# Windowed attention on one core: exponentials by block with row sums, halves of a strip on separate partitions, the normalising product on POOL

## The chip, the cores and the metric

The kernel runs on one NeuronCore of a Trainium2 chip. Its five engines are PE (matrix products), DVE (vector), ACT (activations), POOL (general purpose) and SP (here only a DMA queue). The metric is the device time of one execution in microseconds (us), lower is better.

## The reference, cut to what matters

Input is a batch of 8 images of 56 x 56 tokens with 64 channels. A convolution block, an attention layer, a graph and mixture-of-experts layer follow each other. The change lies in the attention layer alone:

```python
qkv = (x @ W_qkv.T).reshape(Bb, Nn, 3, 8, 8)           # 8 heads of 8 channels
attn = einsum('bhqd,bhkd->bhqk', q, k) * (scale * temperature[0])
mask = local_mask(Nn)                                  # rows and columns at most 3 apart
attn = softmax(where(mask, attn, -inf), axis=-1)
out = einsum('bhqk,bhkd->bhqd', attn, v)
return out @ W_proj.T + b_proj                         # added to the tokens
```

## The kernel before, in words

The program is a row of phases with a barrier between them: `conv_phase`, `attention_phase`, `index_phase`, `table_phase`, `edge_phase`, `join_phase`, `output_phase`. Only `attention_phase` (L787 to L1075) and a mask table are touched.

The phase works through 112 strips (8 images of 14 strips; a strip is 4 rows of 56 tokens). A strip is 14 blocks of 4 x 4 tokens. A block's queries, spread over 8 heads, make 128 rows, and its keys are a window of 10 x 10 = 100 tokens. For each strip:

- SP (`loads`, L869) brings keys, mask features, queries and, in ten transfers, the values.
- POOL (`spread_q`, L898) multiplies the queries by the head mask into `q_exp` (64 x 1792), so that one product gives the scores of all heads of a block. The mask features add -2^100 for keys outside of the window.
- PE (`scores`, L933) writes the scores of 14 blocks to three PSUM banks `psS` (5, 5 and 4 blocks).
- DVE (`subtract_max`, L1025) takes each row's maximum and subtracts it, from PSUM to `prob`, bank by bank. ACT (`exponentials`, L991) takes the exponential of a bank in place.
- PE (`turn_probs`, L947) transposes `prob` block by block to `psP`; ACT (`copy_probs`, L998) copies that to `prob_t`.
- PE (`weigh_values`, L957) multiplies by `val` (100 x 128 for a block: 64 value channels and 64 ones, which give the row sums) to `psO`, in four groups of 4, 4, 4 and 2 blocks. The result holds all heads' products; `own_head` (L1036) on DVE multiplies by the head mask, adds over heads, takes the reciprocal of the sums (L1049) and multiplies (L1052) into `o_ch`.
- PE (`project`, L968) applies the output weights; DVE (`residual`, L1056) adds the tokens; POOL (`add_bias`, L907) adds the bias and stores.

Each engine runs its own program in order, and semaphores join them. What sets the order is each engine's `step`, with i the strip:

```python
pe:   turn_probs(i); scores(i+1); project(i-1); weigh_values(i)
act:  load_t1(i); copy_probs(i); exponentials(i+1)
dve:  subtract_max(i+1); residual(i-1); own_head(i)
pool: spread_q(i+2); add_bias(i-1)
```

`own_head(i)` waits for `weigh_values(i)` group by group. `scores(j)` waits for `spread_q(j)`. `spread_q(j)` waits for `scores(j-2)` and for its queries. fp32 products are issued by the compiler as two instructions on PE each, transposes as one: 28 for the scores, 28 for the values, 14 transposes and 4 for the projection in a strip.

Of the kernel before, what the change touches and what calls it, by code (L numbers as in the profile page):

```python
# [72 lines left out]
def mask_features():  # L73
# [15 lines left out]
    for j in range(QROWS):  # L89
        queries[j, :, :, j, :] = 1  # L90
    for x in range(W):
        queries[QROWS + x % 16, x // QCOLS, :, :, x % QCOLS] = 1
# [694 lines left out]
def attention_phase(nc, io, t1_dram, q_dram, kpad_dram, vpad_dram, t2_dram):  # L787

    with ExitStack() as ctx:
# [8 lines left out]

        ident = sb("a_ident", [128, 128])
        headmask = sb("a_headmask", [2 * C, HEADS])  # L800
        wproj = sb("a_wproj", [C, C])
        bproj = sb("a_bproj", [TOK, C])
# [5 lines left out]
        val = sb2("val", [KEYS, BLOCKS, 2 * C])  # L808
        t1 = sb2("t1", [TOK, 2, C])
        prob = sb2("prob", [128, BLOCKS * KEYS])  # L810
        mx = sb2("mx", [128, BLOCKS])
        prob_t = sb("prob_t", [KEYS, BLOCKS, 128])
        own = sb2("own", [2 * C, 4, HEADS, QB])
        sums = sb("sums", [2 * C, BLOCKS, QB])
        inv = sb("inv", [C, BLOCKS, QB])
        o_ch = sb2("o_ch", [C, SPIX])
        t2a = sb2("t2a", [TOK, 2, C])
        t2 = sb2("t2", [TOK, 2, C])
# [6 lines left out]
        GROUPS = [(0, 4), (4, 8), (8, 12), (12, 14)]  # L825

        const_in = sem("const_in")
        ones_set = sem("ones_set")
# [4 lines left out]
        exp_q = sem("exp_q"); s_ready = sem("s_ready"); mx_done = sem("mx_done"); sub_done = sem("sub_done")  # L833
        exp_done = sem("exp_done"); pt_ready = sem("pt_ready"); pt_done = sem("pt_done")
        pv_ready = sem("pv_ready"); own_done = sem("own_done"); summed = sem("summed"); inv_done = sem("inv_done")
        o_done = sem("o_done"); pr_ready = sem("pr_ready")
        t2a_done = sem("t2a_done"); t2_done = sem("t2_done")

        t1_view = t1_dram.rearrange("(i r p) c -> i p r c", r=2, p=TOK)
        t2_view = t2_dram.rearrange("(i r p) c -> i p r c", r=2, p=TOK)  # L840
        consts = [(ident[:], "ident"), (headmask[0:C], "headmask"), (headmask[C:2 * C], "headmask"), (wproj[:], "wproj")]
# [8 lines left out]
        def every_strip(eng, step):  # L850

            step(Strip(0, 0), True, False)
            step(Strip(0, 1), False, False)
            with eng.Fori(1, PAIRS - 1) as turn:
                step(Strip(turn, 0), False, False)
                step(Strip(turn, 1), False, False)
            step(Strip(PAIRS - 1, 0), False, False)
            step(Strip(PAIRS - 1, 1), False, True)

        with nc.Block() as block:  # L860
            @block.sync
            def _(sp):
                for dst, name in consts:
                    sp.dma_start(dst, io[name]).then_inc(const_in, 16)
                sp.dma_start(bproj[:], io["bproj"].rearrange("(a b) -> a b", a=1).to_broadcast([TOK, C])).then_inc(const_in, 16)
# [3 lines left out]
                def loads(n, s, par, i):  # L869

                    wait(sp, s_ready, 3 * i - 3)
                    sp.dma_start(keys[par][0:C, :],
                                 kpad_dram[:, n, bass.ds(s * QROWS, WIN), :].rearrange("c y x -> c (y x)")).then_inc(kq_loaded[par], 16)
                    sp.dma_start(keys[par][C:KROWS, :], io["kfeat"][bass.ds(s, 1)].rearrange("o f x -> (o f) x")).then_inc(kq_loaded[par], 16)
                    wait(sp, exp_q, i - 1)
                    sp.dma_start(q[par][:], q_dram[:, n, bass.ds(s * SPIX, SPIX)]).then_inc(kq_loaded[par], 16)
                    wait(sp, pv_ready, 4 * i - 4)
                    for ky in range(WIN):
                        sp.dma_start(val[par][ky * WIN:(ky + 1) * WIN, :, 0:C], windows(n, s * QROWS + ky)).then_inc(v_loaded[par], 16)

                sp.wait_ge(ones_set, 2)
                for par in range(2):
                    loads(0, par, par, par)
                with sp.Fori(1, STRIPS // 2) as pair:
                    for par in range(2):
                        loads(0, pair * 2 + par, par, pair * 2 + par)
                with sp.Fori(1, N) as n:
                    with sp.Fori(0, STRIPS // 2) as pair:
                        for par in range(2):
                            loads(n, pair * 2 + par, par, n * STRIPS + pair * 2 + par)  # L890

            @block.gpsimd
            def _(pool):
                for par in range(2):
                    pool.memset(val[par][:], 1.0).then_inc(ones_set, 1)  # L895
                pool.wait_ge(const_in, 16 * N_CONST)

                def spread_q(st):  # L898
# [5 lines left out]
                                       headmask[0:C].unsqueeze(1).unsqueeze(3).to_broadcast([C, BLOCKS, HEADS, QB]),  # L904
                                       ALU.mult).then_inc(exp_q, 1)

                def add_bias(st):  # L907
                    i, par = st.i, st.par
                    pool.wait_ge(t2a_done, i + 1)
                    wait(pool, t2_stored[par], 16 * (st.turn))  # L910
                    pool.tensor_tensor(t2[par][:], t2a[par][:], bproj[:].unsqueeze(1).to_broadcast([TOK, 2, C]), ALU.add)\
                        .then_inc(t2_done, 1)
                    pool.wait_ge(t2_done, i + 1)
                    pool.dma_start(t2_view[i], t2[par][:]).then_inc(t2_stored[par], 16)
# [9 lines left out]
                every_strip(pool, step)  # L924
                add_bias(Strip(PAIRS - 1, 1))
                for par in range(2):
                    pool.wait_ge(t2_stored[par], 16 * PAIRS)

            @block.tensor
            def _(pe):  # L930
                pe.wait_ge(const_in, 16 * N_CONST)

                def scores(st):  # L933
# [3 lines left out]
                    for bank, (a, b) in enumerate(BANKS):  # L937
                        wait(pe, sub_done, 3 * i - 3 + bank + 1)
# [18 lines left out]
                def weigh_values(st):  # L957
                    i, par = st.i, st.par
                    pe.wait_ge(v_loaded[par], 16 * WIN * (st.turn + 1))
                    for k, (a, b) in enumerate(GROUPS):  # L960
                        pe.wait_ge(pt_done, 4 * i + k + 1)
                        wait(pe, own_done, 4 * i + k - 1)
                        for blk in range(a, b):
                            m = pe.matmul(psO[k % 2][:, (blk - a) * 128:(blk - a + 1) * 128], val[par][:, blk, :],  # L964
                                          prob_t[:, blk, :], start=True, stop=True)
                        m.then_inc(pv_ready, 1)

                def project(st):  # L968
# [3 lines left out]
                    for r in range(2):  # L972
                        m = pe.matmul(psM[0:TOK, SPIX + r * C:SPIX + (r + 1) * C], o_ch[par][:, r * TOK:(r + 1) * TOK], wproj[:],
                                      start=True, stop=True)
                    m.then_inc(pr_ready, 1)

                def step(st, first, last):
                    turn_probs(st)
                    if not last:
                        scores(st.step(1))  # L980
# [3 lines left out]

                scores(Strip(0, 0))
                every_strip(pe, step)
# [3 lines left out]
            def _(act):  # L990
                def exponentials(st):  # L991
                    i, par = st.i, st.par
                    for bank, (a, b) in enumerate(BANKS):
                        act.wait_ge(sub_done, 3 * i + bank + 1)
                        p = prob[par][:, a * KEYS:b * KEYS]
                        act.activation(p, p, ACT.Exp).then_inc(exp_done, 1)

                def copy_probs(st):  # L998
                    i, par = st.i, st.par
                    for k, (a, b) in enumerate(GROUPS):  # L1000
                        act.wait_ge(pt_ready, 4 * i + k + 1)
                        if k == 0:
                            wait(act, pv_ready, 4 * i)
# [3 lines left out]
                def load_t1(st):  # L1007
                    i, par = st.i, st.par
                    wait(act, t2a_done, i - 1)
                    act.dma_start(t1[par][:], t1_view[i]).then_inc(t1_loaded[par], 16)  # L1010

                def step(st, first, last):
                    load_t1(st)
                    copy_probs(st)
                    if not last:
                        exponentials(st.step(1))

                exponentials(Strip(0, 0))
                every_strip(act, step)

            @block.vector
            def _(dve):
                dve.wait_ge(const_in, 16 * N_CONST)

                def subtract_max(st):  # L1025
                    i, par = st.i, st.par
                    for bank, (a, b) in enumerate(BANKS):
                        dve.wait_ge(s_ready, 3 * i + bank + 1)
                        s = psS[bank][:, 0:(b - a) * KEYS].rearrange("p (b k) -> p b k", k=KEYS)
                        dve.tensor_reduce(mx[par][:, a:b], s, AX.X, ALU.max).then_inc(mx_done, 1)  # L1030
                        dve.wait_ge(mx_done, 3 * i + bank + 1)
                        dve.tensor_tensor(prob[par][:, a * KEYS:b * KEYS].rearrange("p (b k) -> p b k", k=KEYS), s,
                                          mx[par][:, a:b].unsqueeze(2).to_broadcast([128, b - a, KEYS]), ALU.subtract)\
                           .then_inc(sub_done, 1)

                def own_head(st):  # L1036

                    i, par = st.i, st.par
                    for k, (a, b) in enumerate(GROUPS):
                        n = b - a  # L1040
                        dve.wait_ge(pv_ready, 4 * i + k + 1)
# [929 lines left out]
```

## Time and profile before

| what | value |
|---|---|
| median of 3 runs | 6784.15 us (6781.37 to 6784.29) |
| the profiled execution | 6765.31 us |
| its span in the profile | 6763.6 us |
| PE, DVE, ACT, POOL busy, share of the span | 50%, 55%, 14%, 46% |
| mean granted clock of PE | 0.648 of full speed |
| attention, first `q_exp` to last `t2a` | 1541.9 to 2920.5 us |

The profile gives, for each engine, what it did and what ended each idle time. Its clock column is PE's granted clock as a share of 2.4 GHz: 1.00 is 2.4 GHz and 0.50 is 1.2 GHz. A line number names the line of the kernel that issued an instruction.

### The profile page before, as it was taken

The numbers are of one execution on the slowest core, as the hardware profiler recorded it, in microseconds if no ns is written. First come the engines' busy times: TensorE is split into PE (matmuls) and PEld (weight loads), VectorE is DVE, ScalarE is ACT, GpSimd is POOL, SyncE is SP. The second block draws the span as 40 slices with busy tenths as digits, with TensorE's granted clock in tenths as the row PEclk, the third lists the DMA queues.
The fourth block names the chain that finished last, engine by engine and source line by source line (L and its number), as shares of the span: only waits on it lengthen the run. The fifth ranks groups of instructions, "written<-read, shape, count | busy, mean of one in ns | idle before, by whom it ended". The sixth has DMA issues, their size and how long they took to land. (4 is left out here: it accounts for less than half of the span.)

```text
span 6763.6 us, 59936 instructions
## 1 busy us (share of the span) xinstructions
PE 3366.5 (50%) x16368; PEld 2375.4 (35%) x16368; DVE 3733.1 (55%) x5332; ACT 962.3 (14%) x1813; POOL 3137.9 (46%) x2752
## 2 busy tenths in 40 slices
PE   2788878767888888845444400572222222222000
PEld 0344434336777777734333300341111111111000
DVE  4988888857999999942999400321111111111129
ACT  0112222212333333312000000110000000000000
POOL 0000000003333333312888777677777777777545
PEclk9878787768988989855555555555555555555555
DMA  6455555542222222233100100121111111111125
GB/s 136 81 85 86 85 85 85 84 71 65 63 60 61 60 60 61 60 84 76 31 8 8 20 8 4 56 79 32 32 32 32 32 32 32 30 30 28 25 71 201
DMA packets 551500, 384.17 MB, mean 57 GB/s; under 512 B 370652, under 2 KB 504572, under 8 KB 548452
## 3 DMA queue, kind: packets, MB, share of 16 engines
q1 hardware_dynamic: 357724, 237.30, 13.2%
q10 hardware_dynamic: 116200, 116.30, 9.1%
q0 software_dynamic: 77472, 29.41, 4.4%
q8 instruction: 37, 0.61, 0.0%
q14 instruction: 67, 0.55, 0.0%
HBM read 235.03 MB, written 147.68 MB: 57 GB/s over the span
## 5 line engine op out<-in xcount | busy, mean ns | idle before, releaser
L1406 POOL DMA_INDIRECT e_row<-scratch_table,e_edge x2048 | 2232.4, 1090 | 704.8 <-issue 670.7
L1584 PE MATMUL f_psY<-f_w,f_hid 128*128 128x64 f32 x1568 | 347.3, 423 | 1835.1 <-ACT f_hid L1535 1835.1
L1584 PEld LDWEIGHTS f_psY<-f_w,f_hid 128*128 128x128 f32 x1568 | 338.1, 332 | 1909.9 <-ACT f_hid L1535 1784.6
L1486 DVE TENSOR_TENSOR e_e<-e_row,e_b 128x512 f32<-128x512 f32 x16 | 11.3, 704 | 1321.1 <-DMA e_row<-scratch_table,e_edge 1320.9
L902 POOL TENSOR_TENSOR q_exp<-q,a_headmask 64x1792 f32<-64x1792 f32 x112 | 361.1, 3224 | 798.7 <-DMA q<-scratch_q 798.7
L895 POOL MEMSET val<- 100x1792 f32 x2 | 3.1, 1592 | 1527.6 <-POOLq L137 1527.6
L765 DVE SCALAR_TENSOR_TENSOR acc<-psE,c_b,acc 128x448 f32<-128x448 f32 x840 | 569.0, 677 | 105.7 <-PE psE L458 89.1
L1444 DVE TENSOR_TENSOR i_hot<-i_iota,i_digit 128x1024 bf16<-128x1024 f32 x512 | 581.4, 1207 | 9.5 <-DMA i_before<-in_before 9.5
L964 PE MATMUL psO<-prob_t,val 100*128 100x128 f32 x3136 | 457.3, 296 | 185.2 <-DVE own L1042 185.2
L458 PE MATMUL psE<-stack,c_w 72*128 72x448 bf16 x896 | 387.7, 450 | 308.1 <-DVE acc L765 179.4
L445 PE MATMUL psH<-h,c_w 128*128 128x448 f32 x1008 | 534.2, 618 | 0.9 <-ACT h L548 0.9
L964 PEld LDWEIGHTS psO<-prob_t,val 100*128 100x128 f32 x3136 | 400.6, 203 | 227.0 <-issue 219.1
L1567 PE MATMUL f_psH<-i_hot 128*128 128x128 bf16 x2048 | 264.8, 310 | 326.9 <-DVE i_hot L1444 326.9
L941 PE MATMUL psS<-keys,q_exp 84*128 84x100 f32 x3136 | 410.0, 291 | 25.5 <-POOL q_exp L902 25.5
L1046 DVE TENSOR_REDUCE sums<-own 128x64 f32<-128x512 f32 x448 | 410.0, 915 | 15.4
L941 PEld LDWEIGHTS psS<-keys,q_exp 84*128 84x128 f32 x3136 | 398.6, 209 | 34.9 <-issue 26.9
L1579 PE MATMUL f_psH<-f_z,f_w 64*128 64x512 f32 x392 | 352.4, 1077 | 2.3 <-DVE i_posi L1462 2.3
L458 PEld LDWEIGHTS psE<-stack,c_w 72*128 72x128 bf16 x896 | 95.9, 112 | 685.5 <-DVE acc L765 477.4
L1567 PEld LDWEIGHTS f_psH<-i_hot 128*128 128x128 bf16 x2048 | 197.2, 140 | 394.4 <-DVE i_hot L1444 394.4
L1469 DVE TENSOR_TENSOR f_y<-f_psY,f_b 128x1024 f32<-128x1024 f32 x49 | 59.6, 1216 | 417.8 <-PE f_psY L1584 417.8
L1004 ACT ACTIVATE prob_t<-psP 100x512 f32<-100x512 f32 x448 | 224.3, 541 | 440.4 <-PE psP L953 440.4
L953 PE MATMUL psP<-a_ident,prob 128*100 128x128 f32 x1568 | 275.8, 335 | 17.1 <-ACT prob_t L1004 17.1
(269 smaller groups left out, 5195.1 us busy)
## 6 DMA issues: line engine op xcount, KB each, us to landing
stack<-scratch_parts ACTq DMA_DIRECT2D x504, 112.0 KB
val<-scratch_vpad SPq DMA_DIRECT2D x1120, 35.0 KB
e_row<-scratch_table,e_edge POOLq DMA_INDIRECT x2048
scratch_y<-f_y ACTq DMA_DIRECT2D x49, 512.0 KB, 2.9
g_y<-scratch_y SPq DMA_DIRECT2D x28, 896.0 KB, 4.9
scratch_state<-e_state SPq DMA_DIRECT2D x16, 1536.0 KB, 6.0
scratch_parts<-h2p ACTq DMA_DIRECT2D x56, 336.0 KB, 2.2
keys<-scratch_kpad SPq DMA_DIRECT2D x112, 155.0 KB
```

The lines of the kernel that those rows point to most:

```text
L445: m = pe.matmul(psH2[:, 0:PIX].rearrange("p (y x) -> p y x", x=W), w2[:, tap, :], h1[:, ROWS * t + dy:ROWS * (t + 1) + dy, dx:dx + W], sta ...
L458: pe.matmul(psE[c % 2][:, 0:PIX], w3[:, c, :], stack[SLOT[t]][:, c, :], start=True, stop=True).then_inc(e_ready, 1)
L765: dve.scalar_tensor_tensor(acc[:, SLOT[t]], psE[c % 2][:, 0:PIX], b3[:, c:c + 1], acc[:, SLOT[t]], ALU.max, ALU.add).then_inc(stt_done, 1)
L902: pool.tensor_tensor(q_exp[par][0:C], q[par][:].rearrange("c (b m) -> c b m", m=QB).unsqueeze(2).to_broadcast([C, BLOCKS, HEADS, QB]), hea ...
L941: m = pe.matmul(psS[bank][:, (blk - a) * KEYS:(blk - a + 1) * KEYS], q_exp[par][:, blk].rearrange("k h m -> k (h m)"), keys[par][:].rearra ...
L964: m = pe.matmul(psO[k % 2][:, (blk - a) * 128:(blk - a + 1) * 128], val[par][:, blk, :], prob_t[:, blk, :], start=True, stop=True)
L1046: dve.tensor_reduce(sums[:, a:b, :], own[k % 2][:, 0:n].rearrange("p b h m -> p b m h"), AX.X, ALU.add)\
L1406: pool.indirect_dma_start(out=row[s][:, f, :], out_offset=None, in_=table_dram, in_offset=bass.IndirectOffsetOnAxis(ap=edge[s][:, 0, f:f + ...
L1444: m = dve.tensor_tensor(hot[g % 2][d][:], iota[:].unsqueeze(1).to_broadcast([128, HOT, 128]), digit[par][:, d, g * HOT:(g + 1) * HOT].unsq ...
L1567: m = pe.matmul(psC, hot[g % 2][1][:, c, :], hot[g % 2][0][:, c, :], start=False, stop=False)
L1579: pe.matmul(psH[e][:], w1[:, e, :], z[par][:], start=True, stop=True).then_inc(hid_ready, 1)
L1584: m = pe.matmul(psY[par][:, j, e * C:(e + 1) * C], hid[e][:, j * 128:(j + 1) * 128], w2[:, e, :], start=True, stop=True)
```

## The change

- The signs of queries and masks are turned, so the scores come out negated; the row's minimum (`lowest`) takes the place of the maximum. Nothing is subtracted on DVE any more: ACT computes exp(low - score) from PSUM, one instruction for each of the 14 blocks, with `low` as its bias and the row sum as a second output.
- The reciprocal is taken of 128 x 14 sums (`invert`) and a new step on POOL (`normalise`) multiplies the 128 x 1400 probabilities by it in place, before they are transposed.
- `val` has no ones (64 columns), and `weigh_values` puts blocks 0 to 6 on partitions 0 to 63 and blocks 7 to 13 on 64 to 127 of `psO`, in two parts of 8 and 6 blocks. `own_head` works on both halves at once: 2 products with the head mask, and the heads are added in three pairwise additions.
- `project` is one product with a 128 x 128 weight, where zeros keep the halves apart (112 x 128 out). Loads of tokens and stores of results are two transfers for a strip, not one.
- The scores, their minimum, exponentials and spread queries now run two strips ahead. `turn_probs(i)` waits for the normalised strip, and `weigh_values(i)` for all four copies of the strip.

The orders after it (written as above):

```python
pe:   turn_probs(i); scores(i+2); project(i-1); weigh_values(i)
act:  copy_probs(i); load_t1(i); exponentials(i+2)
dve:  invert(i+1); lowest(i+2); residual(i-1); own_head(i)
pool: normalise(i+1); spread_q(i+2); add_bias(i-2)
```

The diff, cut to its core:

```diff
-                def loads(n, s, par, i):
+                def load_kq(n, s, par, i):
                     wait(sp, s_ready, 3 * i - 3)
...
+                def load_val(n, s, par, i):
+                    wait(sp, pv_ready, 2 * i - 2)
                     for ky in range(WIN):
...
+                def normalise(st):
+                    i, par = st.i, st.par
+                    pool.wait_ge(inv_done, i + 1)
+                    p = prob[par][:].rearrange("p (b k) -> p b k", k=KEYS)
+                    pool.tensor_tensor(p, p, inv[par][:].unsqueeze(2).to_broadcast([128, BLOCKS, KEYS]), ALU.mult).then_inc(norm_done, 1)
...
                 def step(st, first, last):
-                    if not last and not (isinstance(st.turn, int) and st.turn == PAIRS - 1):
-                        spread_q(st.step(2))
+                    if not last or st.par == 0:
+                        normalise(st.step(1))
+                    if not last:
+                        spread_q(Strip(st.turn + 1, st.par))
                     if not first:
-                        add_bias(st.step(-1))
+                        add_bias(Strip(st.turn - 1, st.par))
...
                 def scores(st):
                     pe.wait_ge(exp_q, i + 1)
...
-                        wait(pe, sub_done, 3 * i - 3 + bank + 1)
+                        wait(pe, exp_done, 3 * i - 3 + bank + 1)
...
                 def turn_probs(st):
+                    pe.wait_ge(norm_done, i + 1)
                     for k, (a, b) in enumerate(GROUPS):
-                        pe.wait_ge(exp_done, 3 * i + (1, 2, 3, 3)[k])
...
                 def weigh_values(st):
+                    pe.wait_ge(pt_done, 4 * i + 4)
+                    for part, (a, b) in enumerate(PARTS):
+                        wait(pe, own_done, 2 * i - 2 + part + 1)
+                        for half in range(2):
+                            for blk in range(a, b):
+                                m = pe.matmul(psO[part][half * C:(half + 1) * C, (blk - a) * 128:(blk - a + 1) * 128],
+                                              val[par][:, half * HALF + blk, :], prob_t[:, half * HALF + blk, :], start=True, stop=True)
                         m.then_inc(pv_ready, 1)
...
                 def exponentials(st):
+                    wait(act, pt_ready, 4 * i - 4)
                     for bank, (a, b) in enumerate(BANKS):
+                        act.wait_ge(low_done, 3 * i + bank + 1)
+                        for blk in range(a, b):
+                            m = act.activation(prob[par][:, blk * KEYS:(blk + 1) * KEYS],
+                                               psS[bank][:, (blk - a) * KEYS:(blk - a + 1) * KEYS], ACT.Exp,
+                                               bias=low[par][:, blk:blk + 1], scale=-1.0, accum_out=sums[par][:, blk:blk + 1])
+                        m.then_inc(exp_done, 1)
...
+                def invert(st):
+                    dve.wait_ge(exp_done, 3 * i + 3)
+                    wait(dve, norm_done, i - 1)
+                    dve.reciprocal(inv[par][:], sums[par][:]).then_inc(inv_done, 1)
...
                 def own_head(st):
+                    for part, (a, b) in enumerate(PARTS):
+                        dve.wait_ge(pv_ready, 2 * i + part + 1)
+                        dve.tensor_tensor(own[:, a:b], psO[part][:, 0:(b - a) * 128].rearrange("c (b h m) -> c b h m", h=HEADS, m=QB),
+                                          headmask[:].unsqueeze(1).unsqueeze(3).to_broadcast([2 * C, b - a, HEADS, QB]),
+                                          ALU.mult).then_inc(own_done, 1)
+                    dve.wait_ge(own_done, 2 * i + 2)
+                    dve.tensor_tensor(own[:, :, 0:4], own[:, :, 0:4], own[:, :, 4:8], ALU.add).then_inc(folded, 1)
+                    dve.wait_ge(folded, 2 * i + 1)
+                    dve.tensor_tensor(own[:, :, 0:2], own[:, :, 0:2], own[:, :, 2:4], ALU.add).then_inc(folded, 1)
+                    dve.wait_ge(folded, 2 * i + 2)
...
+                    dve.tensor_tensor(o_ch[par][:].rearrange("c (y b x) -> c b y x", y=QROWS, x=QCOLS), square(0), square(1), ALU.add)\
+                       .then_inc(o_done, 1)
...
                 def step(st, first, last):
+                    if not last or st.par == 0:
+                        invert(st.step(1))
                     if not last:
-                        subtract_max(st.step(1))
+                        lowest(Strip(st.turn + 1, st.par))
                     if not first:
                         residual(st.step(-1))
                     own_head(st)
```

## Rows read from the trace of the kernel before

**Rows 1.** The page: the span, then the granted clock of PE in 40 slices.
```profile
span 6763.6 us, 59936 instructions
...
PEclk9878787768988989855555555555555555555555
```

**Rows 2.** Busy time by stretch: columns PE, PEld, DVE, ACT, POOL, clock, DMA share, GB/s.
```profile
1574.78:2920.23 1345.45, 1137.39 (x8128) 1026.27 (x8128) 1277.17 (x1877) 414.58 (x768) 475.27 (x331) 0.90 0.24 60
```

**Rows 3.** Groups by line and shape, DVE in attention: busy us, mean ns, idle before.
```profile
L1042 DVE TENSOR_TENSOR own<-psO,a_headmask 128x512 f32<-128x512 f32 x336 | 227.8, 678 | 13.1 <-PE psO L964 13.1
L1030 DVE TENSOR_REDUCE mx<-psS 128x5 f32<-128x500 f32 x224 | 150.2, 671 | 51.7 <-PE psS L941 50.5
L1042 DVE TENSOR_TENSOR own<-psO,a_headmask 128x256 f32<-128x256 f32 x112 | 46.0, 411 | 0.0
L1052 DVE TENSOR_TENSOR o_ch<-sums,inv 64x224 f32<-64x224 f32 x112 | 42.9, 383 | 8.6
```

**Rows 4.** What writes t2a: ns min/median/max, first and last start, form.
```profile
L1061 DVE TENSOR_TENSOR t2a<-psM,t x112: 278/280/292, 1574.8 to 2920.2; 112x128 f32<-112x128 f32 x112
```

**Rows 5.** Groups by line and shape, two DVE rows of later phases.
```profile
L1223 DVE TENSOR_TENSOR t_cen<-t_t,t_stat 128x448 f32<-128x448 f32 x28 | 17.5, 626 | 1.0
L1230 DVE RECIPROCAL t_stat<-t_stat 128x7 f32<-128x7 f32 x28 | 5.6, 201 | 114.6 <-ACT t_stat L1273 114.6
```

**Rows 6.** Groups by line and shape, POOL products in this and later phases.
```profile
L902 POOL TENSOR_TENSOR q_exp<-q,a_headmask 64x1792 f32<-64x1792 f32 x112 | 361.1, 3224 | 798.7 <-DMA q<-scratch_q 798.7
L1771 POOL TENSOR_TENSOR g_scaled<-g_y,g_gate 128x1792 f32<-128x1792 f32 x14 | 69.7, 4975 | 105.6 <-DVE g_gate L1851 105.6
L911 POOL TENSOR_TENSOR t<-t2a,a_bproj 112x128 f32<-112x128 f32 x112 | 49.9, 446 | 24.0 <-DVE t2a L1061 24.0
L1241 POOL TENSOR_TENSOR t_z<-t_cen,t_stat 128x448 f32<-128x448 f32 x28 | 26.3, 938 | 146.5 <-DVE t_stat L1230 146.5
```

**Rows 7.** Timeline of PE, a stretch that falls to the lower clock.
```profile
1956.94 1.20 PE L964 MATMUL psO<-prob_t,val 100*128 100x128 f32 x8 [1.78 <-DVE own L1042]
...
1959.59 3.27 PE L953 MATMUL psP<-a_ident,prob 128*100 128x128 f32 x14
1962.65 6.13 PE L941 MATMUL psS<-keys,q_exp 84*128 84x100 f32 x28
1968.72 1.01 PE L973 MATMUL psM<-a_wproj,o_ch 64*112 64x64 f32 x4
1969.65 5.89 PE L964 MATMUL psO<-prob_t,val 100*128 100x128 f32 x28
```

**Rows 8.** Busy time by stretch (columns as in rows 2), around those and the phase's end.
```profile
1971.00:1974.00 3.00, 3.00 (x16) 3.00 (x16) 2.20 (x3) 0.00 (x0) 2.45 (x2) 0.50 0.08 19
1976.00:1978.00 2.00, 1.75 (x15) 1.30 (x14) 1.93 (x4) 1.73 (x4) 0.00 (x0) 1.00 0.20 45
2914.60:2917.00 2.40, 0.00 (x0) 0.00 (x0) 2.33 (x4) 0.00 (x0) 0.00 (x0) 1.00 0.00 0
2917.00:2919.10 2.10, 0.00 (x0) 0.00 (x0) 2.03 (x3) 0.00 (x0) 0.00 (x0) 0.50 0.00 0
```

**Rows 9.** Timeline of PE: the first strip, then a strip at the upper clock.
```profile
1561.09 5.34 PE L964 MATMUL psO<-prob_t,val 100*128 100x128 f32 x28
...
2205.03 1.08 PE L953 MATMUL psP<-a_ident,prob 128*100 128x128 f32 x8
...
2207.15 3.36 PE L941 MATMUL psS<-keys,q_exp 84*128 84x100 f32 x28
2210.44 0.60 PE L973 MATMUL psM<-a_wproj,o_ch 64*112 64x64 f32 x4
2210.97 2.05 PE L964 MATMUL psO<-prob_t,val 100*128 100x128 f32 x16
```

**Rows 10.** Groups by line and shape, ACT.
```profile
L1004 ACT ACTIVATE prob_t<-psP 100x512 f32<-100x512 f32 x336 | 193.6, 596 | 440.4 <-PE psP L953 440.4
L1273 ACT ACTIVATE t_stat<-t_stat 128x7 f32<-128x7 f32 x28 | 5.8, 209 | 7.1 <-DVE t_stat L1228 7.0
```

More of the change, by code:

```diff
@@ L848, in windows, with every_strip, pair @@
             return bass.AP(row.tensor, row.offset, [[C, WIN], [QCOLS * C, BLOCKS], [1, C]])
[L850 to L858, printed above, removed]
+        def every_strip(step):
+            def pair(turn, first, last):
+                step(Strip(turn, 0), first, last)
+                step(Strip(turn, 1), False, last)
+            return pair
         with nc.Block() as block:
@@ L876, in loads, with image @@
                     sp.dma_start(q[par][:], q_dram[:, n, bass.ds(s * SPIX, SPIX)]).then_inc(kq_loaded[par], 16)
-                    wait(sp, pv_ready, 4 * i - 4)
+                def load_val(n, s, par, i):
+                    wait(sp, pv_ready, 2 * i - 2)
                     for ky in range(WIN):
[L879 to L886, printed above, removed]
+                        sp.dma_start(val[par][ky * WIN:(ky + 1) * WIN], windows(n, s * QROWS + ky)).then_inc(v_loaded[par], 16)
+                def image(n):
+                    first = n * STRIPS
+                    load_kq(n, 0, 0, first)
+                    if not (isinstance(n, int) and n == 0):
+                        load_val(n - 1, STRIPS - 1, 1, first - 1)
+                    load_kq(n, 1, 1, first + 1)
+                    load_val(n, 0, 0, first)
+                    with sp.Fori(1, STRIPS // 2) as pair:
+                        for par in range(2):
+                            load_kq(n, pair * 2 + par, par, first + pair * 2 + par)
+                            load_val(n, pair * 2 + par - 1, 1 - par, first + pair * 2 + par - 1)
+                image(0)
                 with sp.Fori(1, N) as n:
-                    with sp.Fori(0, STRIPS // 2) as pair:
-                        for par in range(2):
-                            loads(n, pair * 2 + par, par, n * STRIPS + pair * 2 + par)
+                    image(n)
+                load_val(N - 1, STRIPS - 1, 1, N * STRIPS - 1)
             @block.gpsimd
             def _(pool):
-                for par in range(2):
-                    pool.memset(val[par][:], 1.0).then_inc(ones_set, 1)
+                pool.memset(wproj[:], 0.0).then_inc(zeroed, 1)
                 pool.wait_ge(const_in, 16 * N_CONST)
@@ L971, in project @@
                     wait(pe, t2a_done, i)
[L972 to L975, printed above, removed]
+                    pe.matmul(psM[0:HPIX, 0:2 * C], o_ch[par][:], wproj[:].rearrange("k r c -> k (r c)"),
+                              start=True, stop=True).then_inc(pr_ready, 1)
                 def step(st, first, last):
@@ L979, in step @@
                     if not last:
[L980 removed]
+                        scores(Strip(st.turn + 1, st.par))
                     if not first:
@@ L983, in step @@
                     weigh_values(st)
+                pair = every_strip(step)
                 scores(Strip(0, 0))
-                every_strip(pe, step)
+                scores(Strip(0, 1))
+                pair(0, True, False)
+                with pe.Fori(1, PAIRS - 1) as turn:
+                    pair(turn, False, False)
+                pair(PAIRS - 1, False, True)
                 project(Strip(PAIRS - 1, 1))
```

144 lines of the change are left out of this document (75 added, 69 removed).

## The prediction

> **What bounds the kernel now.** I read the page first for where attention lies and at which clock PE runs [rows 1]: the phase is 1380 of 6763.6 us, slices 10 to 17, and PE's granted clock there is 0.8 to 0.9, while from slice 18 on it is 0.5 whatever is done here. So only attention's own time can change. The busy time of its steady stretch comes next [rows 2]: DVE 1277 of 1345 us (95%), PE 1137 (85%), ACT 415, POOL 475. The write of `t2a`, once in a strip, gives the period: 1345.4 us / 111 = 12.12 us [rows 4]. DVE has 11.5 us of work in it, so DVE is the bound; PE's waits are for DVE [rows 7]. POOL and ACT have 8 us to spare in each strip.
>
> **What the change removes.** From the nearest shapes [rows 3, 5] DVE's work after it is: three minima 1.9 us (two of 0.67, one of 0.56, scaled from it), reciprocal 0.23 (0.20 for 7 columns, a little more for 14), head masks 0.68 + 0.54 (384 columns, between 0.41 and 0.68), three additions 0.63 + 0.38 + 0.28 (448, 224 and 112 columns), residual 0.28. That is 4.9 us for 11.5, some 740 us less DVE work in the phase. If throughput alone counted, this would be a clear gain. It does not count alone, because the orders of the four engines now close a loop through one strip.
>
> **The loop.** Take the end of `weigh_values(i-1)` on PE as zero and follow what PE needs for the end of `weigh_values(i)`:
> 1. DVE runs `own_head(i-1)`: second head mask 0.54, additions 0.63, 0.38 and 0.28 [rows 3 to 5]. Only then, in order, comes `invert(i+1)`, 0.23. Together 2.06 us. Its own inputs, the exponentials of strip i+1, are ready by then (below), so it is late only by its place in DVE's order.
> 2. POOL runs `normalise(i+1)`, 128 x 1400, and behind it in order `spread_q(i+2)`, 3.22 [rows 6]. The spread does not need the normalising; it is queued behind it.
> 3. PE has done `turn_probs(i)`, which takes about 2.1 us at the upper clock [rows 9] and 3.3 at the lower [rows 7]. Its copies on ACT are over by about 4.5 us (four copies of 0.60 or less [rows 10]). Then it waits for `spread_q(i+2)`, and `project(i-1)` and `weigh_values(i)` are queued behind `scores(i+2)`.
> 4. PE runs scores, projection, values: all three in full on the path.
>
> Before, `spread_q(i+2)` ran early, beside DVE's work; in its place it waited only for queries, 799 us in total [rows 6].
>
> **normalise.** No row shows 1400 columns. Low end: the line through 128 columns in 0.446 and 448 in 0.938, the latter with the same broadcast along the last axis [rows 6], gives 2.4 us. High end: 1792 columns of that form in 4.98 [rows 6], 3.9 us by length; DVE ran a product of its own beside a part of that. DVE has little to do while `normalise` runs, but this row is the larger and closer in length: I take 3.0.
> The Trainium skill (GPSIMD Engine Reference, Elementwise side-by-side cycle accounting) has 4497 ns for a sum of 2048 columns; an estimate by length is 3.1 us, and the sum would be 0.1 us a strip higher. The same page (Engine selection) says to use VectorE and not GpSimd for elementwise work; by that rule this product would be on DVE, where rows of before give 1.9 us (1400 columns at 0.68 for 500), and the loop would be 1.1 us shorter.
>
> **PE's clock.** In the loop PE stands still from about 2.5 to 3.5 us until 8.7 us, over 5 us. The trace shows what that does: when the last values ended at 2914.6, the clock was 1.00 until 2917 and 0.50 after, with PE idle [rows 8], and even an idle time of 1.78 us with few products around it came just ahead of a fall [rows 7]. After that fall the clock stayed at 0.50 through transposes and scores and through the first part of the values, and was 1.00 again at 1976 [rows 7, 8]. So I take it that each strip's scores run at 1.2 GHz, and that the clock rises again only late in the values or in the turning behind them, and falls in the next wait. Prices at the lower clock: scores 1962.65 to 1968.72, 6.07 us [rows 7]; two of four projection products, 0.47 of 0.93 (1968.72 to 1969.65); values 5.34 where the clock rose within them [rows 9], 5.89 where that came at their end [rows 7]: 5.6. The new values have 64 weight columns, not 128. Scores move 100 columns and values 128, at the same 0.21 to 0.22 us an instruction at the lower clock, so I can't tell which side sets the pace; ends are 4.0 and 5.9, and I keep 5.6 since the number of instructions and the moved columns stay.
>
> **The sum.** 2.06 + 3.0 + 3.22 + 6.07 + 0.47 + 5.6 = 20.42, and some 0.4 for eight hand-overs of about 0.05 us (an estimate): 20.8 us a strip for 12.12. Over 111 strips that is +966 us. The first strips take about 19 us longer, the last two have no spread and no scores and are some 10 us shorter each: nothing is left of that. The profiled execution of 6765 would become 7731; the median of the runs is 19 us above it, so I forecast 7750.
>
> **What I cost at nothing.** ACT: 14 exponentials of 100 columns. 512 columns cost 0.60 and 7 cost 0.21 [rows 10], so 100 columns about 0.28; the bias pointer and the sum output may add as much again. At 0.54 each they are 7.6 us. They start 3 us after the scores and end by 10.6, while `invert` comes at 13.9 (6.07 + 0.47 + 5.6 + 1.8): covered. Without that cover each 0.1 us more would cost 1.4 us a strip. Both transfers of tokens and both stores lie beside the wait. On POOL `add_bias` follows the spread and has 12 us until the next `invert`. SP's queue: `load_val(i+1)` waits for `weigh_values(i-1)` and has 20 us; `load_kq(i+3)` is queued behind it, and is needed 20 us later. The shorter values' memory, the sign changes and the constants cost nothing that the rows could show.
>
> **Rivals.**
> - PE stays at 2.4 GHz. Against it: the idle time of over 5 us. For it: the clock rose within one strip of work. Scores 3.3, projection 0.3, values 3.6 (16 in 2.05 [rows 9], 28 in proportion) make 15.9 us a strip with the same 8.7 before them: (15.9 - 12.12) x 111 = +420, 7204. Chance 0.10.
> - Faster: the loop does not bind, and PE does. That is so if `spread_q(i+2)` ends before `turn_probs(i)`, 2.1 us after the values. The price is then PE's own work at the upper clock, 2.1 + 3.3 + 0.3 + 3.6 = 9.3, with its dips 9.6: (9.6 - 12.12) x 111 = -280, 6504. Against it: 8.3 us of work of DVE and POOL stand in order before that point. It needs a reading of the two orders that is wrong. Chance 0.04.
> - Halves overlap. `weigh_values` writes two column halves of PE's array. The loop is then shorter by half the values, 2.8 us: -311, 7439. Nothing in the trace shows it, and the kernel issues 16 or 12 instructions for one half before the other. Chance 0.05. The Trainium skill (TensorEngine Tiling, When to Use Tiling) names a stationary side of 64 columns as a case for two column tiles, which would work in parallel.
> - ACT binds: an exponential with its sum costs over 0.78 us and `invert` waits for it. At 1.0 us: 3 + 14 + 0.23 + 3.0 + 3.22 + 0.4 = 23.9 us a strip, 8090. Against it: 512 columns in one instruction cost 0.60 [rows 10], so the second output alone would have to cost 0.4. Chance 0.05.
>
> **Numbers.** My forecast has 0.75. Its bounds: `normalise` 2.4 and values 4.0 give 18.6 us, 7504; `normalise` 3.9, values 5.9 and 0.2 us more of hand-overs give 22.2, 7904. The range 7430 to 7920 also takes in overlapping halves. About 0.2% (14 us) is what a measurement of this kernel can tell from no change. No case lies within it by its mechanism; I leave 0.01. Faster 0.04, same 0.01, slower 0.95.
>
> **What would show it.** Right: the writes of `t2a` 20 to 21 us apart; PE idle for 5 us a strip ahead of the scores with `q_exp` from POOL as the releaser; POOL's `normalise` waiting for `inv`, and that for `own_head`; granted clock below 0.65 in the phase; DVE busy under 30%; the 28 scores in about 6.1 us. Wrong: PE's waits named after `prob` or ACT (then the exponentials or copies bind), a clock near 1.00 (the first rival), or a period under 12 us.

## The result, and the profile after

| | before | after |
|---|---|---|
| median of the runs, us | 6782.76 (4 runs) | 7510.69 (4 runs) |
| ratio after / before | | 1.108, 95% interval 1.106 to 1.110 |
| span of the profiled execution | 6763.6 | 7505.9 |
| first to last write of `t2a` | 1345.4 | 2065.2 |

The kernel is 728 us slower. Forecast were 7750 us and a range of 7430 to 7920. Of the 742 us between the spans, 720 lie between the first and last write of `t2a`, 19.5 ahead of them and 3 behind.

The page of the kernel after: busy time, then two of the rows in 40 slices.

```profile
PE 3646.9 (49%) x16144; PEld 2640.1 (35%) x16144; DVE 2992.2 (40%) x4548; ACT 1294.9 (17%) x4613; POOL 3488.5 (46%) x2975
...
DVE  5988889522222222222329991014111111111119
...
PEclk9787878656666666666555555555555555555555
```

Attention has grown from 8 slices to 11 of a longer span, DVE in it has fallen from 9 tenths to 2, and the granted clock from 0.8 or 0.9 [rows 1] to 0.6. Busy time of the steady stretch (columns as in [rows 2]), and what writes `t2a`:

```profile
1594.30:3659.50 2065.20, 1406.75 (x7894) 1279.80 (x7894) 544.72 (x1100) 734.24 (x3474) 814.46 (x550) 0.64 0.17 39
```

```profile
L1110 DVE TENSOR_TENSOR t2a<-psM,t x112: 282/292/293, 1594.3 to 3659.5; 112x128 f32<-112x128 f32 x112
```

No engine is near its limit: DVE 26%, POOL 39%, PE 68% at a low clock. A mean strip takes 18.6 us (2065.2 / 111) for 12.12 [rows 4]. The waits in that stretch, longest first (who waited, for whom: us, times, longest):

```profile
DVE low L1077 <- PE psS L971: 1182.0, 325, 8.5
POOL prob L923 <- DVE inv L1084: 1168.8, 109, 13.2
ACT prob L1033 <- DVE low L1077: 947.6, 216, 8.8
PEld psS L971 <- issue: 651.1, 108, 6.4
PE psS L971 <- POOL q_exp L914: 624.5, 108, 6.2
```

Every engine waits for another, as in a loop; e1 below tests that it is one. PE's scores wait for POOL's spread in all but a few strips, up to 6.2 us; POOL's normalising product waits for DVE's reciprocal. One turn, from the timeline of all engines (start, length, then what ran):

```profile
2224.10 0.56 DVE L1092 TENSOR_TENSOR own<-psO,a_headmask 128x384 f32<-128x384 f32 x1 [0.52 <-PE psO L995]
2224.69 0.63 DVE L1096 TENSOR_TENSOR own<-own 128x448 f32<-128x448 f32 x1
2225.35 0.39 DVE L1098 TENSOR_TENSOR own<-own 128x224 f32<-128x224 f32 x1
2225.87 0.28 DVE L1102 TENSOR_TENSOR o_ch<-own 128x112 f32<-128x112 f32 x1
2226.06 0.23 DVE L1084 RECIPROCAL inv<-sums 128x14 f32<-128x14 f32 x1
2226.39 2.52 POOL L923 TENSOR_TENSOR prob<-prob,inv 128x1400 f32<-128x1400 f32 x1 [10.79 <-DVE inv L1084]
2228.87 3.21 POOL L914 TENSOR_TENSOR q_exp<-q,a_spreadmask 64x1792 f32<-64x1792 f32 x1
2232.21 6.29 PE L971 MATMUL psS<-keys,q_exp 84*128 84x100 f32 x28 [5.89 <-POOL q_exp L914]
2238.30 0.66 PE L1003 MATMUL psM<-a_wproj,o_ch 128*112 128x128 f32 x2
2238.88 4.16 PE L995 MATMUL psO<-prob_t,val 100*64 100x128 f32 x28
...
2243.08 0.56 DVE L1092 TENSOR_TENSOR own<-psO,a_headmask 128x384 f32<-128x384 f32 x1 [0.59 <-PE psO L995]
```

Read from start to start, the turn is DVE 2.29, POOL 5.82, scores 6.09, projection 0.58, values 4.20: 18.98 us. The 100 writes of `t2a` from 1708.0 to 3585.6 are 18.97 apart. PE's clock in the same strip (columns of a look at PE alone: length, busy, clock, DMA share, GB/s):

```profile
2228.00:2232.00 4.00, 0.00 (x0) 0.84 0.36 82
2232.30:2238.00 5.70, 5.70 (x27) 0.50 0.12 22
2239.00:2242.50 3.50, 3.50 (x27) 0.50 0.00 0
```

PE stands still, the clock falls within the first row (0.84 is a mean over it), and scores and values then run at 0.50, which is 1.2 GHz, in full.

### The profile page after: what moved, and what is told of

Read it like the earlier page. It is cut to its first block and busy times, and to the rows that moved or that the text cites. A ratio compares the mean times of both kernels' runs of the same rounds, so it can differ in the third digit from the quotient of the medians.

```text
span 7505.9 us, 61673 instructions
## 1 busy us (share of the span) xinstructions
PE 3646.9 (49%) x16144; PEld 2640.1 (35%) x16144; DVE 2992.2 (40%) x4548; ACT 1294.9 (17%) x4613; POOL 3488.5 (46%) x2975
## 5 line engine op out<-in xcount | busy, mean ns | idle before, releaser
L971 PE MATMUL psS<-keys,q_exp 84*128 84x100 f32 x3136 | 704.7, 425 | 658.7 <-POOL q_exp L914 658.5
L971 PEld LDWEIGHTS psS<-keys,q_exp 84*128 84x128 f32 x3136 | 677.5, 332 | 686.3 <-issue 678.3
L923 POOL TENSOR_TENSOR prob<-prob,inv 128x1400 f32<-128x1400 f32 x112 | 282.4, 2522 | 1191.9 <-DVE inv L1084 1191.9
L1077 DVE TENSOR_REDUCE low<-psS 128x5 f32<-128x500 f32 x336 | 216.5, 644 | 1244.6 <-PE psS L971 1244.6
L1033 ACT ACTIVATE prob<-psS,low 128x100 f32<-128x100 f32 x1568 | 514.2, 350 | 961.8 <-DVE low L1077 961.8
L995 PE MATMUL psO<-prob_t,val 100*64 100x128 f32 x3136 | 444.6, 415 | 0.5 <-issue 0.5
L995 PEld LDWEIGHTS psO<-prob_t,val 100*64 100x64 f32 x3136 | 406.2, 220 | 28.3 <-issue 28.2
L914 POOL TENSOR_TENSOR q_exp<-q,a_spreadmask 64x1792 f32<-64x1792 f32 x112 | 359.9, 3214 | 10.1 <-DMA q<-scratch_q 10.1
L1600 ACT ACTIVATE e_weight<-e_drop 128x1024 f32<-128x1024 f32 x16 | 16.9, 1056 | 1851.7 <-DVE e_drop L1556 1851.7
```

What stands on the lines that cost most here:

```text
L914: pool.tensor_tensor(q_exp[par][0:C], q[par][:].rearrange("c (b m) -> c b m", m=QB).unsqueeze(2).to_broadcast([C, BLOCKS, HEADS, QB]), spr ...
L971: m = pe.matmul(psS[bank][:, (blk - a) * KEYS:(blk - a + 1) * KEYS], q_exp[par][:, blk].rearrange("k h m -> k (h m)"), keys[par][:].rearra ...
L995: m = pe.matmul(psO[part][half * C:(half + 1) * C, (blk - a) * 128:(blk - a + 1) * 128], val[par][:, half * HALF + blk, :], prob_t[:, half ...
L1033: m = act.activation(prob[par][:, blk * KEYS:(blk + 1) * KEYS], psS[bank][:, (blk - a) * KEYS:(blk - a + 1) * KEYS], ACT.Exp, bias=low[par ...
```

## The experiments

The experiments ran on five chips. On three of them (e1 to e4; e9 and e10; e11) the kernel before took 6775 to 6781 us, on the other two (e5 to e8; e12) 7242 and 7245. The difference of some 460 us lies in the edge phase: from the first gather of `e_row` to the last `e_e` it is 3565 us in e5 and 3109 in the trace of after. 269 us of it are waits of the gathers for `e_edge` (304 against 35 us); why the chips differ was not looked into. Runs are therefore compared by the mean strip, first to last write of `t2a` over 111, and by their ratio to the kernel before on the same chip. Attention itself does not seem to depend on the chip: e6, on a slow one, has the 18.60 us a strip of the changed kernel. e1, e7, e8, e10 and e12 have four runs each, the others one.

| run | strip, us | clock, 1700 to 2500 us | time, us | before there |
|---|---|---|---|---|
| before | 12.12 | 0.90 | 6783 | |
| after | 18.60 | 0.63 | 7511 | 6783 |
| e1 spread first | 11.71 | 0.78 | 6729 | 6781 |
| e2 invert early | 13.70 | 0.70 | 6962 | 6781 |
| e3 short normalise | 16.54 | 0.62 | 7268 | 6781 |
| e4 wide values | 20.09 | 0.67 | 7690 | 6781 |
| e5 PE filled, 16 | 15.87 | 0.84 | 7670 | 7242 |
| e6 keys and queries first | 18.60 | 0.64 | 7971 | 7242 |
| e7 both first | 10.08 | 0.85 | 7023 | 7242 |
| e8 product on DVE | 11.29 | 0.77 | 7155 | 7242 |
| e9 PE filled, 20 | 13.82 | 1.00 | 6989 | 6781 |
| e10 stores on SP | 9.59 | 0.87 | 6491 | 6781 |
| e11 halves in turn | 17.85 | 0.63 | 7438 | 6775 |
| e12 e10 and in turn | 9.58 | 0.85 | 6962 | 7245 |

**e1, the order on POOL.**

```diff
 def step(st, first, last):            # gpsimd
-    if not last or st.par == 0:
-        normalise(st.step(1))
     if not last:
         spread_q(Strip(st.turn + 1, st.par))
+    if not last or st.par == 0:
+        normalise(st.step(1))
```

> POOL's step issues spread_q(i+2) ahead of normalise(i+1); nothing else is changed. Theory (the loop own_head, invert, normalise, spread, scores, values bounds the strip, by the order on POOL): the scores no longer wait for the normalising product. The period falls from 18.6 us to what the busiest engine needs: PE some 9 us at the upper clock, ACT some 8 to 9 (14 exponentials at 0.32 apart, copies 2.1, two issues 1.3). About 9.5 us a strip, the run near 6500 us, below the kernel before too; granted clock over 0.85 in the phase. Rival (the lower clock of PE alone makes it slow, or ACT's 14 exponentials bind): the period stays above 12.1 us and the run above 6780.

Two calls exchanged take 6.9 us off a strip; the ratio to the kernel before is 0.993 (0.990 to 0.995). So the order on POOL was the cause of the loss, and the rival falls: the strip is below 12.12 us. But 9.5 us was not reached, nor a time near 6500. The timeline (PE, SP's queue, POOL) shows why:

```profile
2189.93 3.78 PE L995 MATMUL psO<-prob_t,val 100*64 100x128 f32 x28
...
2193.93 5.24 SPq L886 DMA_DIRECT2D val<-scratch_vpad  x10
...
2199.99 0.48 SPq L876 DMA_DIRECT2D keys<-scratch_kpad  x1
...
2201.29 0.49 SPq L880 DMA_DIRECT2D q<-scratch_q  x1
...
2203.74 3.21 POOL L914 TENSOR_TENSOR q_exp<-q,a_spreadmask 64x1792 f32<-64x1792 f32 x1 [1.79 <-DMA q<-scratch_q]
...
2207.18 6.29 PE L971 MATMUL psS<-keys,q_exp 84*128 84x100 f32 x28 [3.13 <-POOL q_exp L914]
```

POOL now waits for queries. These are issued behind ten value transfers, which wait for PE to be done with the values of the strip two turns back (2189.93 + 3.78). Every second strip has that wait (50 of them from 1600 to 2800, 122.6 us in all), and the scores behind it take 6.29 us, those of the strips between 3.36.

**e2, the order on DVE.** `invert` of strip i+2 goes between `residual` and `own_head`:

```diff
 def step(st, first, last):            # vector
-    if not last or st.par == 0:
-        invert(st.step(1))
     if not last:
         lowest(Strip(st.turn + 1, st.par))
...
+    if not last:
+        invert(Strip(st.turn + 1, st.par))
     own_head(st)
```

> DVE's step inverts the sums of strip i+2 ahead of own_head(i), so that normalise does not wait for the values of the strip before; POOL's order is left. Theory: another loop remains, scores(i+1), exponentials(i+1), invert, normalise, spread, scores(i+2): 8.4 us from the start of the scores to the end of the exponentials at the lower clock (6.4 at the upper), 0.2 + 2.5 + 3.2 and hand-overs. 14.5 us a strip at the lower clock, 12.6 at the upper: 7050 or 6840 us. Rival (the order on DVE is all of it): near 9.5 us a strip, 6500 us. Second rival (it is POOL alone and DVE's order does nothing): 7510 us.

13.70 us, between the two ends given, since strips at the upper clock (values 2.24) and at the lower (4.16) both occur. `own_head` and the values leave the loop, the exponentials enter it: the product waits for the reciprocal 58 times in 800 us, and the reciprocal for ACT as often. So changing DVE's order alone takes 4.9 us off a strip and leaves a shorter loop through POOL's order; changing POOL's alone takes 6.9 off.

**e3, a short normalising product.**

```diff
-    p = prob[par][:].rearrange("p (b k) -> p b k", k=KEYS)
-    pool.tensor_tensor(p, p, inv[par][:].unsqueeze(2).to_broadcast([128, BLOCKS, KEYS]), ALU.mult).then_inc(norm_done, 1)
+    p = prob[par][:, 0:KEYS].rearrange("p (b k) -> p b k", k=KEYS)
+    pool.tensor_tensor(p, p, inv[par][:, 0:1].unsqueeze(2).to_broadcast([128, 1, KEYS]), ALU.mult).then_inc(norm_done, 1)
```

> normalise multiplies only the first of the 14 blocks (100 columns, not 1400), so the probabilities of the other blocks stay unnormalised. Theory: the product lies on the loop in full; 2.52 us become about 0.4, the period 18.6 becomes 16.5, the run about 7275 us. Rival (POOL has slack there and the scores wait for something else): within 30 us of 7510.

16.54 us and 7268: the product falls from 2.52 to 0.35 us, and 2.06 of these 2.17 us come off the strip.

**e4, wide values.**

```diff
-    m = pe.matmul(psO[part][half * C:(half + 1) * C, (blk - a) * 128:(blk - a + 1) * 128],
-                  val[par][:, half * HALF + blk, :], prob_t[:, half * HALF + blk, :], start=True, stop=True)
+    vb = min(half * HALF + blk, BLOCKS - 2)
+    m = pe.matmul(psO[part][:, (blk - a) * 128:(blk - a + 1) * 128],
+                  val[par][:, vb:vb + 2, :].rearrange("k b c -> k (b c)"), prob_t[:, half * HALF + blk, :],
+                  start=True, stop=True)
```

> Each product of weigh_values has 128 stationary columns again (its own block's values and those of the next block), and both halves write all 128 partitions, so the attention output is not the right one. The number of instructions and the 128 moved columns stay. Theory (the stationary columns set the pace of these instructions at the lower clock): 28 instructions take 5.5 to 5.9 us, not 4.16, the period is 20.1 to 20.3 us and the run 7670 to 7700. Rival (it is 4.16 for another reason, for instance because the two halves overlap or the clock differs): 4.2 us and 7510.

```profile
2203.53 5.61 PE L996 MATMUL psO<-prob_t,val 100*128 100x128 f32 x28
```

This row of PE's timeline has 28 instructions in 5.61 us, the value that the prediction took (the mean clock from 2203.6 to 2209.0 was 0.56, so all at 0.50 they would take somewhat longer); with 64 stationary columns the same 28 take 4.16. A strip is 20.09 us, as the theory had it. Since each product now writes all 128 partitions, this run takes away the narrow columns and the separate halves together and can't tell which of them makes the 4.16; e11 can.

**e5 and e9, PE filled.** In the changed order PE gets products of the identity between `turn_probs(i)` and `scores(i+2)`, 16 in e5, 20 in e9:

```diff
     turn_probs(st)
     if not last:
+        pe.wait_ge(pt_done, 4 * st.i + 4)
+        for _ in range(20):
+            pe.matmul(psP[0][:, 0:128], ident[:], ident[:], start=True, stop=True)
         scores(Strip(st.turn + 1, st.par))
```

> Between turn_probs(i) and scores(i+2) PE waits for the four copies of strip i and then does 16 products of the identity with itself into psP, whose results nobody reads; they lie in the time in which PE waits for spread_q. Theory (the loop is what it is, and the lower clock is a consequence of the wait that makes scores, projection and values longer): the granted clock stays near 1.00, the loop has the same 8.1 us ahead of the scores, and behind them 3.3 + 0.35 + 2.3 (values as seen at the upper clock in the first experiment) for 6.1 + 0.6 + 4.1: 14.1 us a strip, the run near 7010. Rival (the clock costs nothing on this path, or the added products delay the scores): 7500 us or more.

> As the filled kernel before, with 20 products in place of 16, so that PE stands still ahead of the scores for some 0.4 us and not 1.1 to 1.4. Theory (the clock still fell once a strip there because of what idle time was left, and that is why its strips took 15.9 us and not 14.1): the clock stays near 1.00 and a strip takes 14.1 to 14.6 us, scores 3.3, values 2.3. Rival (filling can't hold the clock, or the products delay the scores): 15.9 us or more.

With 16 products PE still stood for 0.69 us ahead of them and 0.9 to 1.7 behind, and in most strips the clock fell within the scores (4.1 to 4.3 us, some 3.36), so that the values took 4.16: 15.87 us where 14.1 was expected, a miss, though 2.7 us under the 18.60 of e6 on the same chip. With 20 the mean clock from 1700 to 2500 was 1.00, and 13.82 us came below the 14.1 to 14.6 expected:

```profile
2209.41 4.73 PE L1011 MATMUL psP<-a_ident 128*128 128x128 f32 x40 [0.69 <-ACT prob_t L1047]
2214.40 3.36 PE L971 MATMUL psS<-keys,q_exp 84*128 84x100 f32 x28 [0.26 <-POOL q_exp L914]
2217.60 0.39 PE L1003 MATMUL psM<-a_wproj,o_ch 128*112 128x128 f32 x2
2217.92 2.24 PE L995 MATMUL psO<-prob_t,val 100*64 100x128 f32 x28
```

Work that nobody needs makes the kernel 522 us faster (6989 for 7511), with the loop as it was. That splits the loss, counted in this order: the loop at 2.4 GHz costs 13.82 - 12.12 = 1.70 us a strip (189 us), the lower clock on top of it 18.60 - 13.82 = 4.78 us (531 us). The clock is no second cause, though: it falls in the wait that the loop makes.

**e6 and e7, the order on SP's queue.** Keys and queries of strip j+2 are issued ahead of the values of strip j. e6 has that alone, e7 has it with the spread first.

```diff
     load_kq(n, pair * 2 + par, par, first + pair * 2 + par)
-    load_val(n, pair * 2 + par - 1, 1 - par, first + pair * 2 + par - 1)
+    load_val(n, pair * 2 + par - 2, par, first + pair * 2 + par - 2)
```

> SP's queue issues keys and queries of strip j+2 ahead of the values of strip j, in place of behind the values of strip j. The order on POOL and DVE is that of the changed kernel. Theory (transfers have slack in the changed kernel, the loop over DVE and POOL bounds it): 7510 within 15 us. Rival (queries that come late hold the spread back here too): faster by over 100 us.

> spread_q ahead of normalise on POOL, and keys and queries two strips ahead of the values on SP's queue. Theory (the first experiment stopped at 11.7 us because every second strip's queries were queued behind ten value transfers, which made a loop of 12.9 us and a strip's scores over two strips): that loop goes, PE stays near 2.4 GHz, and the period is what ACT or PE need, 8.8 to 9.4 us; the run near 6430 us. Rival (ACT or PE's clock bound it already): within 60 us of 6729.

e6 changes nothing (18.60 and 18.60): transfers cost nothing while the loop binds. In e7 they do: 10.08 for 11.71 us, a ratio of 0.970 (0.968 to 0.973) to the kernel before. The 8.8 to 9.4 us expected were too low: POOL's own step nearly fills the strip, with its three products 3.24, 2.53 and 0.45, its stores 1.36 with 0.74 of wait, and 1.6 to 1.8 us of wait for the reciprocal.

**e8, the product on DVE.** `normalise` follows `invert` on DVE; SP's queue as in e7.

> The normalising product is done by DVE behind invert, not by POOL, with keys and queries first on SP's queue. Theory: POOL's spread is then not behind it either, so the loop is gone as well; DVE has 4.9 + 1.9 us a strip and is no bound. ACT or PE bound it at 8.8 to 9.4 us, the same as with POOL within 40 us: 6430. Rival (the place on POOL was good for the engine's own sake, since DVE's product delays the minima and own_head): slower than the version with POOL by over 60 us.

```profile
L1081 DVE TENSOR_TENSOR prob<-prob,inv x70: 1616/1618/4597, 1658.1 to 2448.1; 128x1400 f32<-128x1400 f32 x70
```

11.29 us for 10.08: the rival holds. Once the order is mended, the product is better on POOL, though it takes 2.52 us there and mostly 1.62 on DVE. What it delays on DVE was not singled out; PE's turning waits up to 4.0 us for ACT's copies, so that part stays open.

**e10, stores on SP's queue.**

```diff
+    def store(par, i):                # sync, called behind load_val of strip i+4
+        sp.wait_ge(t2_done, i + 1)
+        for r in range(2):
+            sp.dma_start(t2_view[i, :, :, r], t2[par][:, r]).then_inc(t2_stored[par], 16)
...
-    pool.wait_ge(t2_done, i + 1)
-    for r in range(2):
-        pool.dma_start(t2_view[i, :, :, r], t2[par][:, r]).then_inc(t2_stored[par], 16)
```

> Spread first, keys and queries first, and the two stores of a strip are issued on SP's queue, four strips behind the values, in place of POOL's. Theory (POOL is near its limit at 10.1 us a strip: 3.24 + 2.53 + 0.45 + 0.74 + 1.36 = 8.3 and its wait for the reciprocal): POOL has 6.3 us of work, SP 8.0, and a strip takes 9.2 to 9.6 us, bound by ACT and PE. Rival (ACT, or PE's clock, binds at 10.1): no change of the period within 0.15 us. A second rival: SP's queue is now too long, and a strip takes more than 10.1 us.

```profile
POOL q_exp L929 <- DMA q<-scratch_q: 129.6, 71, 5.0
```

9.59 us and 6491 us, 290 below the kernel before (ratio 0.957, 0.956 to 0.959) and 1020 below the changed one: the fastest kernel of the study. The row is of the waits from 1650 to 2450: POOL's wait for queries, absent in e7, is back 71 times, with the stores now ahead of them on SP's queue.

**e11 and e12, halves in turn.** The loops over blocks and halves of `weigh_values` change places, in the changed kernel and in e10.

```diff
-    for half in range(2):
-        for blk in range(a, b):
+    for blk in range(a, b):
+        for half in range(2):
```

> In weigh_values the two halves take turns block by block, in place of 8 (or 6) blocks of one half and then of the other; the rest is the changed kernel. Theory (64 stationary columns make each instruction cheaper at the lower clock, 0.15 us for 0.20, and the halves do not overlap): 28 instructions in 4.1 to 4.2 us, the run within 15 us of 7511. Rival (products for different column halves of the array overlap, and that is where part of the saved time comes from): 2.1 to 3.5 us, a strip shorter by 0.7 to 2 us, 7290 to 7430.

```profile
2218.24 6.29 PE L971 MATMUL psS<-keys,q_exp 84*128 84x100 f32 x28 [5.91 <-POOL q_exp L914]
2224.32 0.65 PE L1003 MATMUL psM<-a_wproj,o_ch 128*112 128x128 f32 x2
2224.91 3.26 PE L995 MATMUL psO<-prob_t,val 100*64 100x128 f32 x28
```

The rival holds: with the halves in turn the same 28 instructions take 3.26 us at a clock of 0.50 (3.10 in the strip before, where it was 0.54), not 4.16. Only the order differs, so work on different column halves of the array does overlap; whether it is two products, or the load of one half beside a product of the other, the run does not tell. In the changed kernel neighbours differ in their half at 3 places of a strip, here at 13. An estimate from that: 0.90 us for 10 more places makes 0.3 us for 3, so most of the step from 5.61 to 4.16 is the narrower stationary side. The run was single; its 73 us are what the rows make of it, 0.75 us a strip.

> The version with the stores on SP's queue (6491 us), with the halves of weigh_values taking turns block by block. Theory (PE and its clock hold part of that version's 9.6 us a strip): the values take 3.1 to 3.3 us at the lower clock and under 2.2 at the upper, a strip is 0.2 to 0.6 us shorter: 6425 to 6470 us. Rival (ACT and the queries' transfers bind it, and less PE work only lowers its clock): within 20 us of 6491, or above it.

In e12 the values take 1.75 us at the upper clock for 2.24, and the strip stays at 9.58 (6962 us, a ratio of 0.962, 0.960 to 0.965, on its chip). Less work for PE left it standing longer (691 of 800 us busy for 715, clock 0.85 for 0.87), so PE's work does not bind e10. The rival holds in that; of what it names instead, the wait for queries is there (132.5 us, 70 times), and a share of ACT was not tested.

## Why the prediction was right, point by point

**The loop** was read from four orders, and each link shows in the trace with the releaser that the prediction named. e1 breaks it by the exchange of two calls, e2 leaves the shorter loop that was worked out for it, and e3 shortens it by nearly what its step lost. Throughput was no guide: DVE's work fell by the 6.6 us a strip that were forecast (545 us busy in the stretch for 1277), and the kernel got slower.

**The clock** fell in the wait and was 0.50 through scores and values, and rose in the turning behind them (1.00 from 2224 to 2226), the second of the two places that the forecast allowed. Its price for the values, 5.6, was taken from rows where the clock rose within them. e9 puts the share of the lower clock at 531 of 720 us. Scores took 6.09 for 6.07, the projection 0.58 for 0.47.

**The size** was right by less than the mechanism. The median of 7511 lies 239 us under the forecast of 7750 and 81 above the low end of the range, and one of the signs given did not come: the writes of `t2a` are 18.97 us apart, not 20 to 21. The other signs came: scores 6.1 us, PE idle over 5 us with `q_exp` as the releaser, a clock of 0.64, DVE 26% busy.

**Terms that were mis-sized.** The values: 5.6 forecast, 4.2 measured, 1.4 us a strip and some 150 us. The prediction could not tell from the trace whether stationary or moved columns set the pace and kept the old price; e4 gives 5.61 with the old columns and e11 shows that overlap of halves is there too. Its low end, 4.0, was the nearer, and the reason given for 5.6, that instructions and moved columns stay the same, was not a sufficient one. The normalising product: 3.0 forecast, 2.52 measured, some 50 us; the line through the two shorter products [rows 6] gave 2.4 and was nearer than the longer one, beside which DVE ran. DVE's steps with their hand-overs took 2.29 us. The ends of the phase were put at nothing: the first strips cost 19.5 us, as said, but the last three writes of `t2a` follow each other at 6.8, 5.7 and 4.7 us and give back 40. Together these are the 225 us between 7731 and 7506 to within 5.

The Trainium skill (GPSIMD Engine Reference, Elementwise side-by-side cycle accounting) led to an estimate of 3.1 us for this product, which took 2.52: the measurement decides. Its rule to use VectorE for elementwise work (Engine selection) fits the instruction, 1.62 us on DVE in e8 for 2.52, but not this kernel's time: e8 against e7, 11.29 to 10.08 us a strip. What the skill says of column tiles working in parallel (TensorEngine Tiling, Key Properties and When to Use Tiling) agrees with e11, 3.26 us for 4.16.

**The rivals.** PE at 2.4 GHz: did not come by itself; made to come in e9 it gives 13.8 us a strip, not the 15.9 worked out, mostly because the values take 2.24 and not 3.6. The faster case needs the loop gone; e1, e7 and e10 reach it by mending the order. That 6491 us is close to the 6504 worked out from PE's own work is luck: PE had 0.87 and not 1.00 of its clock, and in e12 less work for PE changed nothing. Halves overlap: e11 shows that they can, with little effect in the order that the change gives them. The prediction has 16 or 12 instructions for one half before the other; by the code they are 8 or 6, a part of 16 or 12 being both halves. ACT binds: no. An exponential costs 0.35 and its sum output 0.21, but a pair of them passes every 0.32 us: the 14 end at 2221.7, the reciprocal starts at 2226.1.

## What to carry to other kernels

Write out each engine's order and follow every new wait round until it comes back to its own engine: where such a loop closes, its sum bounds the period from below, whatever the engines' busy shares say (here 18.98 us, with no engine over 68%). Put work that others wait for (here the spread of the queries, then keys and queries on the queue) ahead of work that itself waits, and look at the queue order again when the first loop is gone. Where a loop leaves PE standing in each turn, price the products behind the wait at 1.2 GHz too (here 5.9 us of wait, and 0.50 through all scores and values), and give a new shape a range: the values, priced from rows with 128 stationary columns, took 1.4 us less with 64.

## What the runs showed that was not expected

- The fall of PE's clock cost nearly three times as much as the loop at full clock (531 to 189 us), and products without use took 522 us off (e9). Four products fewer (e5) gave 15.87 us a strip for 13.82.
- A sum output of ACT is a second instruction. Both groups of the kernel after, by line (busy us, mean ns):

```profile
L1033 ACT ACTIVATE prob<-psS,low 128x100 f32<-128x100 f32 x1568 | 514.2, 350 | 961.8 <-DVE low L1077 961.8
L1033 ACT ACTIVATION_READ_ACCUMULATOR prob<-psS,low 128x1 f32 x1568 | 332.8, 212 | 0.0
```

- 28 instructions with 64 stationary columns: 4.16 us in the order of the change (8, 8, 6 and 6 of one half), 3.26 with the halves in turn, at the lower clock; 2.24 and 1.75 at the upper (e9, e12). With 128 stationary columns 5.61, nearly all at the lower.
